# Cross attention with both query blocks side by side, and expert weights split into low parts and fetched in smaller steps

## The chip, the cores and the metric

The kernel runs on one core of a Trainium2 chip. The metric is the device time of one launch in microseconds (us). The core has five engines with a queue each: PE (TensorE, matrix products and transposes), DVE (VectorE), ACT (ScalarE), POOL (GpSimd) and SP (SyncE, which here only issues DMAs). Every engine works its queue in the written order and waits on semaphores.

## The reference

One decoder layer on x of 16 sequences x 256 rows x 256 columns, all in float32. It has three parts, each followed by a layer norm: a linear attention with decay, a cross attention against 77 context rows, and a mixture of experts in which every row uses 2 of 8 experts.

```python
x = _layernorm(x + _L0_attn_ref(x, ...))
x = _layernorm(x + _L0_xattn_ref(x, ctx_1024, ctx_1024, mask, ...))
x = _layernorm(x + _L0_ffn_ref(x, router_w, gate_w, gate_b, up_w, up_b, down_w, down_b))

...
scores = jnp.einsum('bhqd,bhkd->bhqk', qh, kh) * scale
scores = jnp.where(mask[:, None, :, :] == 0, jnp.float32(-1000000000.0), scores)
probs = jax.nn.softmax(scores, axis=-1)
out = jnp.einsum('bhqk,bhkd->bhqd', probs, vh)
...
g = jnp.einsum('nd,edf->nef', xf, gate_w) + gate_b
u = jnp.einsum('nd,edf->nef', xf, up_w) + up_b
h = jax.nn.silu(g) * u
expert_out = jnp.einsum('nef,efd->ned', h, down_w) + down_b
y = jnp.einsum('ne,ned->nd', probs, expert_out)
```

## The kernel before

The program has five stages that follow one another: `linear_attention` (to about 750 us), `cross_attention` (to about 1036 us), `route_tokens`, `run_experts` (about 1070 to 1475 us) and `combine`. The order of the work is written by hand: in each stage every engine has a function `sequence` or `tile` that says in which order it takes its steps, and semaphores tie the engines together. The change touches two stages.

**cross_attention.** One turn of `sequence(b, ...)` works on one of 16 sequences b, and each sequence has two blocks of 128 query rows (`blk` 0 and 1). The work of a sequence is spread over neighbouring turns. The steps for one block, and the engine that does them:

- PE `turn_x1` transposes the input rows and ACT `keep_xT` (L992) copies the result out of PSUM. PE `project_q` (L1242) makes the queries, ACT `keep_q` (L999) keeps them.
- PE `score` (L1258) makes the scores of one block in `ps_s`, of which there is one buffer. DVE `keep_scores` takes them out in four operations (L1125), adding the mask, and takes the row maximum (L1131).
- POOL `shift` (L955) subtracts the maximum, ACT `exponentials` (L1005) takes exp, DVE `sums` (L1136, L1138) makes the sum and its reciprocal, POOL `weigh` (L960) multiplies by it. All four pass over 128 x 1232 numbers. POOL also makes the mask bias (`mask_to_bias`, L947).
- PE `turn_probs` (L1273) transposes the ten chunks of the block in groups 0, 1 and 2 of 4, 4 and 2 chunks, through two PSUM buffers, and ACT `keep_pT` (L1014) copies each group.
- For both blocks at once: PE `weigh_values` (L1286), ACT `keep_oT` (L1021), PE `project_o` (L1294), DVE `add_residual` and `statistics`, ACT `normalise` (L1026 to L1040), PE `turn_x2` (L1305), ACT `keep_x2T` (L1048), PE `route` (L1312), ACT `keep_logits` (L1052).

Before the change the two blocks are half a turn apart: block 0 of sequence b+1 goes through score, shift and exp in turn b, block 1 in turn b+1. SP's `load_k`, `load_x`, `load_mask`, `load_v`, `store_x2` and `load_residual` are issued once a turn and are not touched.

**run_experts.** The rows are sorted by expert into tiles: 16 tiles of 512 rows, then 7 of 256 rows, the short tiles. Each tile has one expert. float32 products are made of three products of high and low parts, so each weight matrix is split: ACT `gu_high` (L1777) copies gate and up into the high part, POOL `low_parts` (L1757) subtracts it from the raw weights (128 x 2048 numbers, two SBUF inputs). ACT `dn_high` and DVE `dn_low` do the same for the down weights, ACT `x_high` and DVE `x_low` (L1833) for the input rows, ACT `hid_high` and DVE `hid_low` (L1868, two SBUF inputs) for the hidden layer. In tile t, PE does `gate_up(t, 0)` and `gate_up(t, 1)` (L1934), `down(t-1)` (L1946), `turn_x(t+1)` (L1923), `gate_up(t, 2)` and `gate_up(t, 3)`. `gate_up(t+1, 0)` waits for `low_parts` and `x_low` of tile t+1.

There are two buffers of raw weights. In tile t SP waits until both low parts of tile t are made, then reads the number of the expert of tile t+2 from a table (`experts`, L1694 and the value loads behind it), and then issues three loads of 512 KB (L1701 twice, L1703), which all count up one semaphore. `gu_high` waits for all three:

```python
act.wait_ge(w_loaded[par], 16 * W_LOADS * (turn + 1))
```

Of the kernel before, what the change touches and what calls it, by code (L numbers as in the profile page):

```python
# [14 lines left out]
P = 128  # L15
# [724 lines left out]
def cross_attention(nc, sh, cross, x1_dram, x1_bo_dram, mask, x2_dram, x2_all, logits_all):  # L740
# [18 lines left out]
    with ExitStack() as ctx:  # L759
# [165 lines left out]
        def _(pool):  # L925
# [49 lines left out]
            shift(0, 0, 0)  # L975
            all_sequences(pool, sequence)

        @block.scalar
        def _(act):
# [74 lines left out]
            def sequence(b, par, turn):  # L1054
                if has(b, 1):
                    keep_xT(b + 1)
                if has(b, -1):
                    keep_pT(b - 1, 1 - par, 1, (0, 1))
                if has(b, -2):
                    normalise(b - 2)  # L1060
                if has(b, -1):
                    keep_pT(b - 1, 1 - par, 1, (2,))
                if has(b, 1):
                    keep_q(b + 1)
                exponentials(b, par, 1)
                if has(b, -1):
                    keep_oT(b - 1)
                keep_pT(b, par, 0, (0, 1))
                if has(b, -2):
                    keep_x2T(b - 2)  # L1070
                keep_pT(b, par, 0, (2,))
                if has(b, -2):
                    keep_logits(b - 2)
                if has(b, 1):
                    exponentials(b + 1, 1 - par, 0)
# [8 lines left out]
            exponentials(0, 0, 0)  # L1084
            all_sequences(act, sequence)
            keep_pT(B - 1, (B - 1) % 2, 1, range(NG))
            normalise(B - 2)
            keep_x2T(B - 2)
            keep_logits(B - 2)
            keep_oT(B - 1)  # L1090
# [5 lines left out]
        def _(vec):  # L1096
# [75 lines left out]
            for c in range(1, B // SEQS):  # L1172
                for t in range(KC):
                    keep_k(c, t)
            all_sequences(vec, sequence)
# [4 lines left out]
        def _(pe):  # L1180
# [135 lines left out]
            def sequence(b, par, turn):  # L1316
                if has(b, 1):
                    turn_x1(b + 1)
                if has(b, -1):
                    turn_probs(b - 1, 1 - par, 1, (0, 1))  # L1320
                if has(b, 1):
                    project_q(b + 1)
                if has(b, -1):
                    turn_probs(b - 1, 1 - par, 1, (2,))
# [3 lines left out]
                turn_probs(b, par, 0, (0, 1))  # L1328
                if has(b, -2):
                    turn_x2(b - 2)  # L1330
                turn_probs(b, par, 0, (2,))
                if has(b, -1):
                    project_o(b - 1)
                if has(b, -2):
                    route(b - 2)
                if has(b, 1):
                    score(b + 1, 1 - par, turn + par, 1)
# [795 lines left out]
```

## Time and profile before

| what | us |
|---|---|
| median of 3 runs | 1579.49 |
| lowest and highest | 1578.34, 1579.90 |
| the profiled execution | 1584.93 |
| its span, first to last instruction | 1583.2 |

Over the span PE is busy for 83%, PE's weight loads 71%, DVE 55%, ACT 56% and POOL 45%. The profiled execution is one more run of the same program. A row of the timeline gives the start, the time in us, the engine, the line, the operation, what it writes and reads, and how many instructions are merged in it; in brackets stands how long the engine was idle before it, and what ended that. PE's matmuls overlap, so how long PE spends on a step is best read from one step's start to the next one's.

### The profile page before, as it was taken

What the parts mean: (1) busy time and instruction counts of PE and PEld (TensorE: products, weight loads), DVE (VectorE), ACT (ScalarE), POOL (GpSimd) and SP (SyncE); (2) the same over time, 40 slices, a digit from 0 to 9 for tenths busy, and PEclk for the clock granted to TensorE, in tenths of its full rate; (3) what the DMA queues carried; (4) which work ended last, traced back from release to release, by engine and by line L of the source; (5) the groups of instructions that cost most, each with busy time, mean ns of one, the idle gap of its engine ahead of it and who ended that gap; (6) DMA issues with size and microseconds to landing.
All of it is one profiled execution on the core that took longest, in us unless ns stands there. A gap on an engine that the chain in (4) does not pass through costs nothing. (4 is left out here: it accounts for less than half of the span.)

```text
span 1583.2 us, 30994 instructions
## 1 busy us (share of the span) xinstructions
PE 1321.9 (83%) x10439; PEld 1119.0 (71%) x10439; DVE 874.0 (55%) x1806; ACT 887.7 (56%) x2018; POOL 713.8 (45%) x792
## 2 busy tenths in 40 slices
PE   5999999999999999997879889713899999998100
PEld 4788888888888888885667667503789888888100
DVE  3345455545444545554577787567455555566446
ACT  4677777777777777775256666500454554555101
POOL 2244444444444444445266666401544445354564
PEclk9999999999999999998889999955899999999655
DMA  3300000000000000001133332202444544555333
GB/s 126 75 15 28 21 28 28 28 22 28 28 18 25 28 21 28 21 22 48 51 74 82 102 99 75 76 13 91 143 144 160 174 153 139 176 175 147 93 117 122
DMA packets 127907, 120.61 MB, mean 76 GB/s; under 512 B 42498, under 2 KB 108650, under 8 KB 127786
## 3 DMA queue, kind: packets, MB, share of 16 engines
q1 hardware_dynamic: 120970, 100.42, 20.7%
q0 software_dynamic: 6816, 18.62, 4.3%
q8 instruction: 70, 1.15, 0.3%
q14 instruction: 51, 0.42, 0.1%
HBM read 83.93 MB, written 28.26 MB: 71 GB/s over the span
## 5 line engine op out<-in xcount | busy, mean ns | idle before, releaser
L293 POOL TENSOR_SCALAR_AFFINE_SELECT a_decay<-a_decay 128x256 f32<-128x256 f32 x256 | 114.7, 452 | 260.6 <-ACT a_decay L373 258.9
L496 DVE TENSOR_TENSOR a_probs<-a_ps_s,a_decay 128x384 f32<-128x384 f32 x256 | 131.5, 552 | 158.5 <-PE a_ps_o L676 147.4
L302 POOL TENSOR_TENSOR a_key_sum<-a_probs 128x256 f32<-128x256 f32 x128 | 94.2, 736 | 170.3 <-DVE a_probs L496 158.2
L336 ACT ACTIVATE a_qk_exp<-a_ps_qk 128x512 f32<-128x512 f32 x128 | 76.5, 598 | 137.9 <-PE a_ps_qk L582 130.5
L582 PE MATMUL a_ps_qk<-a_xT_hi,a_w_hi 128*128 128x256 f32 x512 | 144.7, 283 | 3.6 <-ACT a_qk_relu L337 3.6
L582 PE MATMUL a_ps_qk<-a_xT_hi,a_w_lo 128*128 128x256 f32 x512 | 143.9, 281 | 0.0
L582 PE MATMUL a_ps_qk<-a_xT_lo,a_w_hi 128*128 128x256 f32 x512 | 143.7, 281 | 0.0
L1757 POOL TENSOR_TENSOR e_gu_lo<-e_gu_raw,e_gu_hi 128x2048 fp32r<-128x2048 f32 x23 | 106.4, 4627 | 81.8 <-ACT e_gu_hi L1777 81.8
L489 DVE SCALAR_TENSOR_TENSOR a_qk<-a_qk_exp,a_qk_relu 128x512 f32<-128x512 f32 x128 | 89.0, 695 | 97.4 <-ACT a_qk_relu L337 97.4
L657 PE MATMUL a_ps_s<-a_qk 64*128 64x256 f32 (+1 forms) x1024 | 132.2, 338 | 0.7 <-DVE a_probs L496 0.4
L1750 POOL DMA_INDIRECT e_x_in<-x_rows,e_index x78 | 74.8, 959 | 121.2 <-DVE e_index L1853 104.2
L371 ACT ACTIVATE a_decay<-a_ps_c,a_c_now 128x256 f32<-128x256 f32 x256 | 124.2, 485 | 2.4 <-PE a_ps_c L647 1.5
L1804 ACT CAST e_hid_hi<-e_hid 128x512 fp32r<-128x512 f32 (+1 forms) x92 | 49.1, 554 | 126.1 <-PE e_ps_y L1946 84.0
L670 PE MATMUL a_ps_o<-a_probs,a_values 128*64 128x256 f32 (+1 forms) x1024 | 111.5, 339 | 0.4 <-DVE a_probs L496 0.4
L657 PEld LDWEIGHTS a_ps_s<-a_qk 64*128 64x128 f32 x1024 | 107.8, 187 | 2.5 <-issue 2.4
L582 PEld LDWEIGHTS a_ps_qk<-a_xT_hi,a_w_hi 128*128 128x128 f32 x512 | 97.7, 191 | 5.4 <-issue 5.3
L955 POOL TENSOR_TENSOR b_probs<-b_probs,b_top 128x1232 f32<-128x1232 f32 x32 | 72.6, 2269 | 62.4 <-DVE b_top L1131 62.3
L373 ACT ACTIVATE a_decay<-a_ps_c,a_c_now 128x128 f32<-128x128 f32 x256 | 98.2, 384 | 0.0
L582 PEld LDWEIGHTS a_ps_qk<-a_xT_hi,a_w_lo 128*128 128x128 f32 x512 | 98.1, 192 | 0.0
L582 PEld LDWEIGHTS a_ps_qk<-a_xT_lo,a_w_hi 128*128 128x128 f32 x512 | 97.8, 191 | 0.1
L1862 DVE SCALAR_TENSOR_TENSOR e_hid<-e_ps_u,e_bias,e_gate 128x512 f32<-128x512 f32 (+1 forms) x92 | 61.1, 669 | 63.3 <-ACT e_gate L1798 55.3
L307 POOL TENSOR_TENSOR a_oT_lo<-a_oT,a_oT_hi 128x256 fp32r<-128x256 f32 x128 | 93.9, 734 | 1.2 <-ACT a_oT_hi L390 1.2
(282 smaller groups left out, 4024.3 us busy)
## 6 DMA issues: line engine op xcount, KB each, us to landing
e_gu_raw<-in_L_ffn_gate_w SPq DMA_DIRECT2D x23, 512.0 KB
e_gu_raw<-in_L_ffn_up_w SPq DMA_DIRECT2D x23, 512.0 KB
e_dn_raw<-in_L_ffn_down_w SPq DMA_DIRECT2D x23, 512.0 KB
y_sorted<-e_y_out SPq DMA_DIRECT2D x16, 512.0 KB
a_x_in<-in_x SPq DMA_DIRECT2D x16, 256.0 KB, 2.7
a_x_res<-in_x SPq DMA_DIRECT2D x16, 256.0 KB, 2.7
x_rows<-a_x SPq DMA_DIRECT2D x16, 256.0 KB, 2.1
x_bo_rows<-a_x_bo SPq DMA_DIRECT2D x16, 256.0 KB, 2.1
```

The source lines that it names most:

```text
L293: pool.affine_select(out=d, in_=d, compare_op=ALU.is_ge, fill=0.0, base=0, pattern=[[0, 2], [1, P]], channel_multiplier=-1)\
L302: pool.tensor_tensor(key_sum[:], probs[:, :, P:N], probs[:, :, N:TRI], ALU.add).then_inc(keys_summed, 1)
L307: pool.tensor_tensor(oT_lo[g % 2][:], oT[g % 2][:], oT_hi[g % 2][:].bitcast(F32), ALU.subtract).then_inc(oT_lo_done, 1)
L336: act.activation(qk_exp[:], ps_qk[:], ACT.Exp)
L371: act.activation(decay[h][:, 0:N], ps_c[:, h, :], ACT.Exp, bias=c_now[:, 0, head:head + 1], scale=-1.0)
L373: act.activation(decay[h][:, N:TRI], ps_c[:, h, P:N], ACT.Exp, bias=c_now[:, 1, head:head + 1], scale=-1.0).then_inc(decay_exp[h], 1)
L489: vec.scalar_tensor_tensor(qk[g][:], qk_exp[:], 1.0, qk_relu[:], ALU.min, ALU.add).then_inc(qk_done, 1)
L496: vec.tensor_tensor(probs[:, h, :], ps_s[h][:, 0:TRI], decay[h][:], ALU.mult)\
L582: mm = pe.matmul(out, l, r, start=(n == 0), stop=(n == len(todo) - 1))
L657: mm = pe.matmul(ps_s[h][:, out], qk[g][rows, 1, j], qk[g][rows, 0, i], start=True, stop=True)
L670: pe.matmul(out[h][:, 0, cols], values[par][:, j, 2 * g + h, :], probs[:, h, keys], start=(j == 0), stop=(j == 1), skip_group_check=True)
L1757: pool.tensor_tensor(gu_lo[par][:], gu_raw[par][:], gu_hi[par][:].bitcast(F32), ALU.subtract)\
```

## The change

In `cross_attention` both blocks of a sequence take each softmax step in the same turn, one right behind the other. `shift(b+1, 0)` and `shift(b+1, 1)` stand behind `weigh(b, 1)` on POOL, both `exponentials(b, ...)` stand in turn b on ACT, both `keep_scores(b+1, ...)` stand together on DVE. PE and ACT get a new order, in which the transposes of a block's probabilities are cut at another place, and `project_o(b-1)` stands between the two `score` steps. At the end of the stage `project_o(B-1)` and `keep_oT(B-1)` move ahead of the last steps of sequence B-2.

In `run_experts` the low parts of gate and up are made in four operations of 128 x 512, the table is read ahead of the waits, gate and up are loaded after their own low part is made and down after its own, and gate/up and down have semaphores of their own. `dn_high` now waits for the down weights. The pieces of the diff below are, in this order: POOL's and DVE's turn in the cross attention, PE's end of that stage, and in `run_experts` POOL's low parts, SP's tile, and ACT's two copies.

```diff
             def sequence(b, par, turn):
-                shift(b, par, 1)
                 weigh(b, par, 0)
                 weigh(b, par, 1)
                 if has(b, 1):
                     shift(b + 1, 1 - par, 0)
+                    shift(b + 1, 1 - par, 1)
                 if has(b, 2):
                     mask_to_bias(b + 2, par)
...
             def sequence(b, par, turn):
-                keep_scores(b, par, 1)
                 sums(b, par, 0)
                 sums(b, par, 1)
                 if has(b, 1):
                     keep_scores(b + 1, 1 - par, 0)
+                    keep_scores(b + 1, 1 - par, 1)
...
             turn_probs(B - 1, (B - 1) % 2, 1, range(NG))
             weigh_values(B - 1, (B - 1) % 2, (B - 1) // 2)
+            project_o(B - 1)
             turn_x2(B - 2)
             route(B - 2)
-            project_o(B - 1)
...
-                pool.tensor_tensor(gu_lo[par][:], gu_raw[par][:], gu_hi[par][:].bitcast(F32), ALU.subtract)\
-                    .then_inc(gu_lo_done[par], 1)
+                for k in range(KC):
+                    for cols in (slice(0, FF), slice(FF, 2 * FF)):
+                        ins = pool.tensor_tensor(gu_lo[par][:, k, cols], gu_raw[par][:, k, cols],
+                                                 gu_hi[par][:, k, cols].bitcast(F32), ALU.subtract)
+                ins.then_inc(gu_lo_done[par], 1)
...
                 if has(t, 2):
+                    e_next, e = experts(t, 1, 2, t + 2)
                     sp.wait_ge(gu_lo_done[par], turn + 1)
+                    load_gate_up(e, par)
                     sp.wait_ge(dn_lo_done[par], turn + 1)
-                    e_next, e = experts(t, 1, 2, t + 2)
-                    load_weights(e, par)
+                    load_down(e, par)
...
-                act.wait_ge(w_loaded[par], 16 * W_LOADS * (turn + 1))
+                act.wait_ge(gu_loaded[par], 16 * GU_LOADS * (turn + 1))
...
+            def dn_high(t, par, turn):
+                act.wait_ge(dn_loaded[par], 16 * (turn + 1))
```

PE's queue for one whole turn of the cross attention, before. `b_ps_m` takes `turn_x1`, `project_q`, `turn_x2` and `route`, `b_ps_s` the scores, `b_ps_t` the transposed probabilities (of block 0 or 1), `b_ps_o` first `weigh_values` and then `project_o`:

```order
L1235 MATMUL b_ps_m<-ident,b_x_in 128x128 x4
L1273 MATMUL b_ps_t<-ident,b_probs_1 128x128 x8
L1242 MATMUL b_ps_m<-b_xT,b_wT 128x256 x4
L1273 MATMUL b_ps_t<-ident,b_probs_1 128x128 x2
L1286 MATMUL b_ps_o<-b_pT,b_v_now 64x256 x12
L1258 MATMUL b_ps_s<-b_k_now,b_qT 128x154 x8
L1273 MATMUL b_ps_t<-ident,b_probs_0 128x128 x8
L1305 MATMUL b_ps_m<-ident,b_x 128x128 x4
L1273 MATMUL b_ps_t<-ident,b_probs_0 128x128 x2
L1294 MATMUL b_ps_o<-b_wT,b_oT 128x256 x4
L1312 MATMUL b_ps_m<-b_rwT,b_x2T 128x8 x4
L1258 MATMUL b_ps_s<-b_k_now,b_qT 128x154 x8
```

The same turn of PE's queue now:

```order
L1275 MATMUL b_ps_t<-ident,b_probs_1 128x128 x4
L1237 MATMUL b_ps_m<-ident,b_x_in 128x128 x4
L1275 MATMUL b_ps_t<-ident,b_probs_1 128x128 x6
L1244 MATMUL b_ps_m<-b_xT,b_wT 128x256 x4
L1288 MATMUL b_ps_o<-b_pT,b_v_now 64x256 x12
L1260 MATMUL b_ps_s<-b_k_now,b_qT 128x154 x8
L1296 MATMUL b_ps_o<-b_wT,b_oT 128x256 x4
L1275 MATMUL b_ps_t<-ident,b_probs_0 128x128 x4
L1260 MATMUL b_ps_s<-b_k_now,b_qT 128x154 x8
L1307 MATMUL b_ps_m<-ident,b_x 128x128 x4
L1275 MATMUL b_ps_t<-ident,b_probs_0 128x128 x6
L1314 MATMUL b_ps_m<-b_rwT,b_x2T 128x8 x4
```

The count of matmuls is the same. All transposes of block 1 of the sequence before now stand ahead of `project_q`, and the score of block 1 stands in the middle of the turn instead of at its end, with `project_o` between the two scores.

ACT's queue in the first part of a turn, before (`b_pT` is `keep_pT`, 4x128 or 2x128 by group; the rows to L1040 are `normalise`):

```order
L992 COPY b_xT<-b_ps_m 128x512
L1014 COPY b_pT<-b_ps_t 128x4x128 x2
L1026 ACTIVATE b_ln_var<-b_mv,b_eps_col 128x2
L1028 ACTIVATE b_rstd<-b_ln_var 128x2
L1030 ACTIVATE b_minus_rstd<-b_rstd 128x2
L1033 ACTIVATE b_shift<-b_mv,b_minus_rstd 128x1 x2
L1040 ACTIVATE b_x<-b_resid,b_shift,b_rstd 128x256 x2
L1014 COPY b_pT<-b_ps_t 128x2x128
L999 ACTIVATE b_qT<-b_ps_m,b_bq_col 128x256 x2
L1005 ACTIVATE b_probs_1<-b_probs_1 128x16x77
L1021 COPY b_oT<-b_ps_o 128x512
```

And now:

```order
L1015 COPY b_pT<-b_ps_t 128x4x128
L993 COPY b_xT<-b_ps_m 128x512
L1015 COPY b_pT<-b_ps_t 128x4x128
L1006 ACTIVATE b_probs_0<-b_probs_0 128x16x77
L1015 COPY b_pT<-b_ps_t 128x2x128
L1006 ACTIVATE b_probs_1<-b_probs_1 128x16x77
L1000 ACTIVATE b_qT<-b_ps_m,b_bq_col 128x256 x2
L1022 COPY b_oT<-b_ps_o 128x512
L1027 ACTIVATE b_ln_var<-b_mv,b_eps_col 128x2
```

Both exps stand between the copies of the transposed probabilities and `keep_q`; `normalise` moved from ahead of `keep_q` to behind `keep_oT`. Before, the exp of block 0 was the last step of the turn before.

## Rows read from the trace of the kernel before

**Rows 1.** Busy time by stretch, two turns of cross attention: us, engines (instructions), PEclk, DMA, GB/s

```profile
870.50:885.00 14.50, 12.13 (x109) 9.36 (x104) 11.00 (x20) 9.29 (x20) 9.76 (x5) 1.00 0.34 94
885.00:899.85 14.85, 12.93 (x103) 9.79 (x103) 10.96 (x19) 9.58 (x21) 9.79 (x6) 0.89 0.32 91
```

**Rows 2.** Timeline of PE over one turn of cross attention: start, us, step

```profile
914.46 0.81 PE L1258 MATMUL b_ps_s<-b_k_now,b_qT 32*128 32x154 f32 x16
...
918.44 1.99 PE L1242 MATMUL b_ps_m<-b_xT,b_wT 128*128 128x256 f32 x8 [1.71 <-ACT b_xT L992]
...
920.58 3.04 PE L1286 MATMUL b_ps_o<-b_pT,b_v_now 128*64 128x256 f32 x24
923.55 0.81 PE L1258 MATMUL b_ps_s<-b_k_now,b_qT 32*128 32x154 f32 x16
...
925.90 1.89 PE L1294 MATMUL b_ps_o<-b_wT,b_oT 128*128 128x256 f32 x8
...
928.51 0.81 PE L1258 MATMUL b_ps_s<-b_k_now,b_qT 32*128 32x154 f32 x16
```

**Rows 3.** PE's waits in ten turns: total us, times, longest us

```profile
PE b_ps_m L1242 <- ACT b_xT L992: 16.2, 10, 2.2
```

**Rows 4.** Costliest groups of cross attention: busy us, mean ns, idle before

```profile
L955 POOL TENSOR_TENSOR b_probs<-b_probs,b_top 128x1232 f32<-128x1232 f32 x32 | 72.6, 2269 | 62.4 <-DVE b_top L1131 62.3
L1125 DVE SCALAR_TENSOR_TENSOR b_probs<-b_ps_s,b_mask_bias 128x308 f32<-128x308 f32 x128 | 52.1, 470 | 9.2 <-PE b_ps_s L1258 5.4 <-PE b_ps_t L1273 2.5 <-issue 0.6
...
L1131 DVE TENSOR_REDUCE b_top<-b_probs 128x16 f32<-128x1232 f32 x32 | 45.9, 1436 | 1.1
...
L1005 ACT ACTIVATE b_probs<-b_probs 128x1232 f32<-128x1232 f32 x32 | 39.9, 1246 | 43.8 <-POOL b_probs L955 43.8
...
L999 ACT ACTIVATE b_qT<-b_ps_m,b_bq_col 128x256 f32<-128x256 f32 x32 | 13.4, 470 | 3.3 <-PE b_ps_m L1242 3.3
```

**Rows 5.** Timeline: second score of sequences 1 and 15, PE at the end

```profile
797.61 1.64 DVE L1125 SCALAR_TENSOR_TENSOR b_probs<-b_ps_s,b_mask_bias 128x308 f32<-128x308 f32 x4
...
1004.10 1.63 DVE L1125 SCALAR_TENSOR_TENSOR b_probs<-b_ps_s,b_mask_bias 128x308 f32<-128x308 f32 x4
...
1017.84 2.81 PE L1286 MATMUL b_ps_o<-b_pT,b_v_now 128*64 128x256 f32 x24
...
1023.72 3.50 PE L1294 MATMUL b_ps_o<-b_wT,b_oT 128*128 128x256 f32 x8 [0.75 <-ACT b_oT L1021]
```

**Rows 6.** Timeline of PE: starts of short tiles 17, 18 and 22

```profile
1400.99 0.36 PE L1934 MATMUL e_ps_g<-e_xT_hi,e_gu_hi 128*128 128x256 f32 x1
...
1412.60 0.55 PE L1934 MATMUL e_ps_g<-e_xT_hi,e_gu_hi 128*128 128x256 f32 x1 [2.44 <-DVE e_hid L1862]
...
1458.33 0.36 PE L1934 MATMUL e_ps_g<-e_xT_hi,e_gu_hi 128*128 128x256 f32 x1 [2.56 <-DVE e_hid L1862]
```

**Rows 7.** Timeline of short tile 17: SP, ACT, POOL, DVE

```profile
1404.29 0.75 SPq L1694 DMA_DIRECT2D e_where<-tile_table  x1
1407.53 0.39 SPq L1701 DMA_DIRECT2D e_gu_raw<-in_L_ffn_gate_w  x1
...
1404.00 1.91 ACT L1777 CAST e_gu_hi<-e_gu_raw 128x2048 fp32r<-128x2048 f32 x1 [1.39 <-DMA e_dn_raw<-in_L_ffn_down_w]
...
1406.09 4.61 POOL L1757 TENSOR_TENSOR e_gu_lo<-e_gu_raw,e_gu_hi 128x2048 fp32r<-128x2048 f32 x1 [4.04 <-ACT e_gu_hi L1777]
...
1407.77 3.56 DVE L1868 TENSOR_TENSOR e_hid_lo<-e_hid,e_hid_hi 128x256 fp32r<-128x256 f32 x2
```

**Rows 8.** Timeline of POOL: two operations back to back

```profile
889.96 2.27 POOL L955 TENSOR_TENSOR b_probs<-b_probs,b_top 128x1232 f32<-128x1232 f32 x1 [1.85 <-DVE b_top L1131]
892.19 2.27 POOL L960 TENSOR_TENSOR b_probs<-b_probs,b_rden 128x1232 f32<-128x1232 f32 x1
```

**Rows 9.** The page's costliest groups: a POOL operation of 256 columns

```profile
L302 POOL TENSOR_TENSOR a_key_sum<-a_probs 128x256 f32<-128x256 f32 x128 | 94.2, 736 | 170.3 <-DVE a_probs L496 158.2
```

**Rows 10.** Timeline of DVE ahead of the first tile

```profile
1085.72 6.26 DVE L1899 TENSOR_SCALAR e_col_hot<-e_count,slot_col,e_number 128x78 fp32r<-128x78 f32 x8
```

More of the change, by code:

```diff
@@ L975, in _ @@
             shift(0, 0, 0)
+            shift(0, 0, 1)
             all_sequences(pool, sequence)
@@ L1054, in sequence @@
             def sequence(b, par, turn):
+                if has(b, -1):
+                    keep_pT(b - 1, 1 - par, 1, (0,))
                 if has(b, 1):
@@ L1057, in sequence @@
                 if has(b, -1):
-                    keep_pT(b - 1, 1 - par, 1, (0, 1))
+                    keep_pT(b - 1, 1 - par, 1, (1,))
+                exponentials(b, par, 0)
+                if has(b, -1):
+                    keep_pT(b - 1, 1 - par, 1, (2,))
+                exponentials(b, par, 1)
+                if has(b, 1):
+                    keep_q(b + 1)
+                if has(b, -1):
+                    keep_oT(b - 1)
                 if has(b, -2):
                     normalise(b - 2)
[L1061 to L1068, printed above, removed]
+                keep_pT(b, par, 0, (0,))
                 if has(b, -2):
                     keep_x2T(b - 2)
-                keep_pT(b, par, 0, (2,))
+                keep_pT(b, par, 0, (1, 2))
                 if has(b, -2):
                     keep_logits(b - 2)
-                if has(b, 1):
-                    exponentials(b + 1, 1 - par, 0)
             keep_xT(0)
@@ L1083, in _ @@
             keep_q(0)
-            exponentials(0, 0, 0)
             all_sequences(act, sequence)
             keep_pT(B - 1, (B - 1) % 2, 1, range(NG))
+            keep_oT(B - 1)
             normalise(B - 2)
@@ L1089, in _ @@
             keep_logits(B - 2)
-            keep_oT(B - 1)
             normalise(B - 1)
@@ L1174, in _ @@
                     keep_k(c, t)
+            keep_scores(0, 0, 1)
             all_sequences(vec, sequence)
@@ L1316, in sequence @@
             def sequence(b, par, turn):
+                if has(b, -1):
+                    turn_probs(b - 1, 1 - par, 1, (0,))
                 if has(b, 1):
@@ L1327, in sequence @@
                     score(b + 1, 1 - par, turn + par, 0)
-                turn_probs(b, par, 0, (0, 1))
+                if has(b, -1):
+                    project_o(b - 1)
+                turn_probs(b, par, 0, (0,))
+                if has(b, 1):
+                    score(b + 1, 1 - par, turn + par, 1)
                 if has(b, -2):
                     turn_x2(b - 2)
-                turn_probs(b, par, 0, (2,))
-                if has(b, -1):
-                    project_o(b - 1)
+                turn_probs(b, par, 0, (1, 2))
                 if has(b, -2):
                     route(b - 2)
-                if has(b, 1):
-                    score(b + 1, 1 - par, turn + par, 1)
             turn_x1(0)
@@ L1731, in _ @@
             e0, e1 = experts(0, 0, 2, 1)
-            load_weights(e0, 0)
-            load_weights(e1, 1)
+            load_gate_up(e0, 0)
+            load_down(e0, 0)
+            load_gate_up(e1, 1)
+            load_down(e1, 1)
             sp.wait_ge(table_ready, 1)
@@ L1814, in tile @@
                     x_high(t + 1, 1 - par)
-                    dn_high(t + 1, 1 - par)
+                    dn_high(t + 1, 1 - par, turn + par)
                 for f in range(2, FC):
@@ L1822, in _ @@
             gu_high(0, 0, 0)
-            dn_high(0, 0)
+            dn_high(0, 0, 0)
             x_high(0, 0)
```

15 lines of the change are left out of this document (7 added, 8 removed).

## The prediction

> **What bounds the kernel now.** I began with the busy time by stretch. PE is filled in the linear attention and in the tiles of 512 rows. It is not filled in the cross attention and in the short tiles, which are the two places the change touches. In the cross attention a turn takes 14.5 us, or 14.85 us where the granted clock of the stretch is 0.89, while DVE works 11.0 us, POOL 9.8 and ACT 9.3 to 9.6 of it [rows 1]. So no engine is full, and a chain across engines must set the turn. PE's own timeline shows how much PE needs. From one second score to the next are 928.51 - 914.46 = 14.05 us, of which 1.71 us are a wait [rows 2]. What is left is 12.34 us: 2.27 (score, input rows, 8 transposes), 2.14 (queries, 2 transposes), 2.97 (values), 2.35 (score, 10 transposes, x2), 2.61 (output projection, routing). The wait is on `keep_xT`, and it stands in each of ten turns, 16.2 us in all [rows 3]. `keep_xT` is not late by itself: it stands on ACT behind the exp of block 0, which waits for POOL's `shift`, which waits for DVE's maximum [rows 4].
>
> In the short tiles PE starts tile 17 at 1400.99 and tile 22 at 1458.33, 57.34 / 5 = 11.47 us a tile [rows 6]. PE works 1412.60 - 2.44 - 1400.99 = 9.17 us of tile 17 and then waits. Three things are late in it [rows 7]. ACT's `gu_high` waited 1.39 us for the last weight load, the down weights, which it does not read. SP issued the loads only 3.24 us after it asked for the expert's number (1404.29 to 1407.53). And two `hid_low` operations took 3.56 us: they ended when POOL's `low_parts` had ended (1406.09 + 4.61 = 1410.70), and `x_low`, for which PE waits, stands behind them on DVE. The row at PE names DVE's `e_hid`; the semaphores behind it are those of `x_low`.
>
> **Cross attention, the new turn.** No instruction is added. I followed the new queues through two turns with the durations of the rows. Two limits compete.
>
> The first is the softmax loop, from the score of block 0 through both blocks to the score of the next sequence: score 0.81 [rows 2], DVE block 0 1.63 [rows 5] and 1.44, DVE block 1 again 3.07, `shift` of block 1 2.27, its exp 1.25, `keep_q` 2 x 0.47 [rows 4]. The sum is 11.4 us; I put some 0.1 us on each hand-over, about 11.9. Sums and reciprocals run beside the other block, and DVE's 11.0 us of work also fit. POOL's mask now stands between `shift` and `weigh`, 0.8 us that lie under DVE's sums.
>
> The second is PE's 12.34 us. It is larger, so PE should become the bound. What hides PE's former wait: ACT now copies the input rows ahead of the exps, and the six transposes of groups 1 and 2 stand between `turn_x1` and `project_q`. What is late next: `project_o` asks for `keep_oT` right behind the score, `project_q` for `keep_xT`, `route` for `keep_x2T`, and the last values for the copy of group 2, behind one exp. I count 0.05 to 0.1 us at each, 0.3 together, which makes 12.65. `keep_q` is queued behind two exps, but PE has 2.97 us of values to do meanwhile. SP's queue is not touched: its 12 value loads wait for `weigh_values` once a turn, as before, and in rows 3 no DMA is among what PE waits for.
>
> The clock: in a stretch at 0.89 a turn that PE bounds would grow by 12.34 x (1/0.89 - 1) = 1.5 us. In the view of rows 1 such turns are four of thirteen, and in the one shown PE works more, not less, than its neighbour. I take half as many, since PE will pause less, 0.2 us a turn. So 12.8 us a turn, bounded by 12.34 (no wait at all) and 13.8 (the waits that I count as covered come out at half of what goes away now).
>
> Before, the second scores of sequences 1 and 15 stand 1004.10 - 797.61 = 206.5 us apart, 14.75 a turn [rows 5]. Saved: 14 x (14.75 - 12.8) = 27.3 us (13.3 to 33.7). The first turns stay: `keep_q` of sequence 1 comes some 3 us later, but DVE is not free for the score before about then.
>
> At the end of the stage the last `project_o` starts at 1023.72, though its input was there at 1017.84 + 2.81 = 1020.65 plus a copy [rows 5]. It can start 2.4 us earlier. The `normalise` behind it now meets that of sequence 14 on ACT. I take 2 us (0 to 3).
>
> **Experts.** Four operations in place of one: 2048 columns cost 4.61 [rows 7], 256 columns 0.736 [rows 9], so 2.16 ns a column and 0.18 us each. A piece is 1.29 us, four are 5.16: 0.55 us more on POOL. In the large tiles nothing waits for it. There the change is at nothing, as long as DVE's `hid_low` does not meet POOL.
>
> In a short tile `gu_high` could start at 1404.00 - 1.39 = 1402.61, 1.6 us into the tile [rows 7]. Then 1.91 for the copy, 0.18 to POOL, 5.16: the low parts are ready 8.9 us into the tile, or 9.7 if DVE's two operations cut in between. That is near PE's 9.17. The other path: `hid_low` comes 1407.77 - 1400.99 = 6.8 us into the tile, and waits for one piece or two rather than for all. Unheld it would end at about 7.6, at the latest with POOL's last piece at 9.7. From its end to PE's next tile it was 1412.60 - 1411.33 = 1.27 us, so 8.9 to 11.0. The number's 3.2 us of reading fall away ahead of the loads, so these go out that much earlier. I take 9.8 us a tile, the middle of the two paths: 5 x (11.47 - 9.8) = 8.3 us, bounded by 9.17 (11.5 us) and by 11.0 (2.3 us).
>
> The Trainium skill speaks for and against this. Its page "SBUF — State Buffer" (section "SBUF: two separate sides") says that GpSimd and a DVE operation with two SBUF inputs take a shared port pair as an exclusive lock for a whole instruction. The 3.56 us of rows 7 agree. By that rule four instructions give four places to get in, which is the forecast. Its page "GPSIMD Engine Reference" (section "2.1 Instruction dispatch") says that a core begins the next instruction as soon as it has done its share of the last. If so the pair might never be let go between pieces, which is the second rival below. By the first page the time is the forecast's, by the second that rival's.
>
> Ahead of the first tile DVE's eight small operations took 6.26 us under the first `low_parts` [rows 10]. They would be held 0.6 us longer by four pieces, and this chain sets the first tile: -0.3 to +0.9, I take +0.6.
>
> **Sum.** -27.3 - 2 - 8.3 + 0.6 = -37.0 us. The profiled execution took 1584.93, so 1547.9 for one like it. The median of the runs, 1579.49, lies 5.4 us below it, and 1579.49 - 37.0 = 1542.5.
>
> **Rivals.**
>
> 1. The hand-overs hold PE. If `keep_q` or `keep_oT`, behind two exps on ACT, is late, PE waits again and the turn stays at 13.8 us. For it: ACT works in order and now has both exps in one piece. Against it: the 2.97 us of values. Saved: 14 x 0.95 + 2 + 8.3 - 0.6 = 23.0, so 1556.5.
>
> 2. The pieces don't let DVE in. Two POOL operations follow one another without a gap: the second starts at 892.19, the first ends at 889.96 + 2.27 = 892.23 [rows 8]. If `hid_low` is held to the end of all four at 8.9, it ends 1411.33 - 1410.70 = 0.6 us later, and the tile takes 8.9 + 0.6 + 1.3 = 10.8 us. Experts then save 5 x 0.67 = 3.4 us rather than 8.3, and the time is 1547.4. The change would then not do what its split says, and only the earlier loads would pay.
>
> 3. Slower. PE is the bound, so its clock decides. The last output projection, at the lower level, took 3.50 us where one in the loop took 1.89 [rows 2, 5], so a whole turn at that level would take 12.34 x 0.85 = 10.5 us more. If 26% of the denser turns' time fell to it, a mean granted clock of 0.87, they would lose 14 x 0.26 x 10.5 = 38 us, the whole gain. That is the point from which it decides; at a mean of 0.84 the time is about 1587. Against it: the full-clock stretches of rows 1 have PE as busy as those at 0.89.
>
> 4. Both go better than I count: 12.4 us a turn, 9.2 a tile, 1579.49 - 32.9 - 2 - 11.4 + 0.6 = 1533.8.
>
> **How the numbers follow.** Forecast 0.50, rival 1 0.16, rival 2 0.16, rival 3 0.04, rival 4 0.11, and 0.03 for a turn that stays as it is. A difference of 0.2% (3 us) is about what a measurement of this kernel can tell from none. Faster by more: 0.94. Within: 0.02. Slower: 0.04. The range from 1532 to 1558 takes in the forecast, rivals 1, 2 and 4.
>
> **What would show it.** In the profile of the changed kernel, second scores of DVE 12.6 to 13.0 us apart, PE's wait on `keep_xT` gone or under 0.3 us a turn, and PEclk 0.95 or more in the stage. In the short tiles, starts 9.8 us apart, `gu_high` no longer released by a DMA, `hid_low` for two blocks under 2.5 us. Turns over 13.5 us mean that a chain I held covered is not, and PE's waits name it. `hid_low` at 3 us or more with four POOL pieces beside it means rival 2.

## The result and the profile after

The changed kernel took 1543.44 us (median of 4 runs, 1540.89 to 1545.17), the kernel before 1578.91 us (median of 4): a ratio of 0.9776, 95% interval 0.9758 to 0.9794, or 35.5 us less; the forecast was 37.0 us less. In a later comparison the ratio was 0.9763 (0.9749 to 0.9776), 37.0 us less.

The profiled execution took 1540.89 us, with a span of 1539.0. Against the span before, 1583.2, that is 44.2 us. Walking down both traces from mark to mark, the difference splits as follows.

| stretch | before | after | difference | forecast |
|---|---|---|---|---|
| second score of sequence 1 to that of sequence 15 | 206.5 | 176.6 | -29.9 | -27.3 |
| from there to the last logits | 31.3 | 28.0 | -3.3 | -2 |
| last logits to the first rows transposed for the experts | 75.7 | 75.4 | -0.4 | +0.6 (with the next row) |
| tile 0, first to third block of gate and up | 8.0 | 9.2 | +1.2 | |
| start of tile 17 to start of tile 22 | 57.3 | 52.0 | -5.3 | -8.3 |
| tile 22 to the last output of the experts | 15.5 | 15.1 | -0.4 | 0 |
| combine, which the change does not touch | 105.7 | 101.0 | -4.7 | 0 |
| ahead of the second score of sequence 1 | 797.6 | 796.2 | -1.4 | 0 |

The stretches that the table leaves out, from the third block of tile 0 to tile 17 above all, agree within 0.1 us. The last two rows can't be put down to the change (see the end). Without them the traces differ by 38.1 us.

**Cross attention.** Three turns by stretch in the changed kernel, and the whole stretch of 14 turns, with the columns of [rows 1] (us, then PE, PEld, DVE, ACT, POOL busy, the granted clock, the DMA share, GB/s):

```profile
858.91:871.61 12.70, 12.62 (x110) 9.61 (x109) 10.90 (x21) 9.69 (x21) 9.78 (x5) 1.00 0.40 107
871.61:884.28 12.67, 12.62 (x110) 9.61 (x109) 10.90 (x20) 9.80 (x21) 9.78 (x5) 1.00 0.40 108
884.28:896.96 12.68, 12.61 (x110) 9.61 (x109) 10.91 (x21) 9.69 (x21) 9.79 (x5) 1.00 0.40 108
796.24:972.88 176.64, 175.00 (x1489) 133.40 (x1490) 151.37 (x262) 133.10 (x283) 137.00 (x70) 0.99 0.37 99
```

PE is busy for 175.0 of 176.6 us. DVE and POOL work what they worked in [rows 1]; the turn around them is shorter, and no turn after the first falls to the lower clock that [rows 1] show at 0.89. PE's timeline over one turn shows no wait in brackets, where [rows 2] had 1.71 us:

```profile
880.20 0.81 PE L1260 MATMUL b_ps_s<-b_k_now,b_qT 32*128 32x154 f32 x16
880.95 1.99 PE L1296 MATMUL b_ps_o<-b_wT,b_oT 128*128 128x256 f32 x8
...
888.20 1.99 PE L1244 MATMUL b_ps_m<-b_xT,b_wT 128*128 128x256 f32 x8
890.13 2.81 PE L1288 MATMUL b_ps_o<-b_pT,b_v_now 128*64 128x256 f32 x24
892.87 0.41 PE L1260 MATMUL b_ps_s<-b_k_now,b_qT 32*128 32x154 f32 x4
```

From score to score it is 892.87 - 880.20 = 12.67 us. What is left of the waits stands at PE's weight loads. These are the totals over 820 to 970 us (us, times, longest us), against 16.2 us in ten turns of [rows 3]:

```profile
PEld b_ps_m L1244 <- ACT b_xT L993: 3.3, 12, 0.3
PEld b_ps_m L1314 <- ACT b_x2T L1049: 3.1, 12, 0.3
PEld b_ps_o L1296 <- ACT b_oT L1022: 2.1, 12, 0.2
```

**Short tiles.** Starts of tiles 17, 18, 19 and 22 on PE (answers to [rows 6]):

```profile
1367.29 0.36 PE L1946 MATMUL e_ps_g<-e_xT_hi,e_gu_hi 128*128 128x256 f32 x1
...
1377.70 0.36 PE L1946 MATMUL e_ps_g<-e_xT_hi,e_gu_hi 128*128 128x256 f32 x1 [1.35 <-DVE e_hid L1874]
...
1388.11 0.35 PE L1946 MATMUL e_ps_g<-e_xT_hi,e_gu_hi 128*128 128x256 f32 x1 [1.35 <-DVE e_hid L1874]
...
1419.29 0.36 PE L1946 MATMUL e_ps_g<-e_xT_hi,e_gu_hi 128*128 128x256 f32 x1 [1.28 <-DVE e_hid L1874]
```

That is 10.41 us a tile, where it was 11.47. PE still waits 1.35 us in each. Tile 18 on ACT, POOL and DVE (answers to [rows 7]):

```profile
1379.24 1.91 ACT L1788 CAST e_gu_hi<-e_gu_raw 128x2048 fp32r<-128x2048 f32 x1
...
1381.32 5.24 POOL L1767 TENSOR_TENSOR e_gu_lo<-e_gu_raw,e_gu_hi 128x512 fp32r<-128x512 f32 x4 [1.79 <-ACT e_gu_hi L1788]
...
1384.03 1.37 DVE L1880 TENSOR_TENSOR e_hid_lo<-e_hid,e_hid_hi 128x256 fp32r<-128x256 f32 x1
...
1385.07 1.49 POOL L1767 TENSOR_TENSOR e_gu_lo<-e_gu_raw,e_gu_hi 128x512 fp32r<-128x512 f32 x1
1385.33 1.52 DVE L1880 TENSOR_TENSOR e_hid_lo<-e_hid,e_hid_hi 128x256 fp32r<-128x256 f32 x1
...
1386.84 0.74 DVE L1845 TENSOR_TENSOR e_xT_lo<-e_ps_x,e_xT_hi 128x256 fp32r<-128x256 f32 x2
1387.50 0.47 DVE L1874 SCALAR_TENSOR_TENSOR e_hid<-e_ps_u,e_bias,e_gate 128x256 f32<-128x256 f32 x1
```

`gu_high` waits for nothing and starts 1.54 us into the tile. POOL's four pieces (one row together; the last of them also by itself, from 1385.07) end at 1382.6, 1383.9, 1385.1 and 1386.6. The first `hid_low` starts 0.2 us behind the second of these ends and is let go by the third, the second `hid_low` by the fourth; each ends 0.28 us behind the end that lets it go. Each takes 1.4 to 1.5 us instead of 0.43. Behind them stand `x_low` and `hidden(2)`, and PE starts 0.14 us after `hidden(2)` ends (1387.97 to 1388.11).

### The profile page after: what moved, and what is told of

Its sections match the earlier page's. It is cut to its first block and busy times, and to the rows that moved or that the text cites. A ratio compares the mean times of both kernels' runs of the same rounds, so it can differ in the third digit from the quotient of the medians.

```text
span 1539.0 us, 31104 instructions
## 1 busy us (share of the span) xinstructions
PE 1315.0 (85%) x10439; PEld 1110.6 (72%) x10439; DVE 873.6 (57%) x1806; ACT 890.7 (58%) x2018; POOL 726.5 (47%) x861
## 5 line engine op out<-in xcount | busy, mean ns | idle before, releaser
L1767 POOL TENSOR_TENSOR e_gu_lo<-e_gu_raw,e_gu_hi 128x512 fp32r<-128x512 f32 x92 | 117.3, 1305 | 72.2 <-ACT e_gu_hi L1788 72.2
L1874 DVE SCALAR_TENSOR_TENSOR e_hid<-e_ps_u,e_bias,e_gate 128x512 f32<-128x512 f32 (+1 forms) x92 | 61.0, 668 | 57.3 <-ACT e_gate L1810 45.7
```

The lines of the kernel that those rows point to most:

```text
L1767: ins = pool.tensor_tensor(gu_lo[par][:, k, cols], gu_raw[par][:, k, cols], gu_hi[par][:, k, cols].bitcast(F32), ALU.subtract)
```

## The experiments

Each kernel was compared with the kernel before on its own chip. Three groups of four shared a chip, on which the kernel before took 1565.99, 1567.81 and 1581.34 us. Between groups only ratios and stretches of the traces are compared. Unless said otherwise an edit is made in the changed kernel.

### The two parts alone

`cross_only` is the kernel before with the new `cross_attention`, `experts_only` the kernel before with the new `run_experts`.

> Only the cross attention is changed; the experts are those of the kernel before. Theory (the two parts do not touch each other): second scores of DVE 12.6 to 12.7 us apart, the end of the stage 3.3 us shorter, in all 33 us less than before in the median (about 1546), short tiles still 11.5 us a tile. Rival (the gain in the cross attention is partly given back in the experts when these stay as before, or the other way round): a saving under 30 us, and this kernel together with experts_only does not add up to the whole change.

> Only the experts are changed; the cross attention is that of the kernel before. Theory: short tiles 10.4 us apart rather than 11.47 (5 times 1.06 = 5.3 us), the first tile about 0.8 us later, so 4.5 us less than before (about 1574). Rival (the 4.7 us by which the combine was shorter in the trace of the changed kernel belong to the change, for instance through an earlier last store): 9 us less (about 1570), with the combine shorter in its trace too.

Measured: `cross_only` 1536.52 us, ratio 0.9811 (0.9795 to 0.9826), 29.5 us less; `experts_only` 1562.31 us, ratio 0.9971 (0.9960 to 0.9982), 3.7 us less. In the traces the turns of `cross_only` are 12.61 us, the stretch to the last logits is 28.2, and those logits come 32.5 us earlier than in `experts_only`, whose turns are 14.76 us. The two savings add up to 33.2 us, where the whole change saved 35.5 and 37.0. Each has some 2 us of uncertainty, so the times show no more than that the parts are independent within it; "under 30 us" was just met, but the sum does not fail. The traces are sharper. From the second score of sequence 1 to the last logits `cross_only` takes 204.7 us and the changed kernel 204.6; from there to the last output of the experts `cross_only` takes 438.3 us and the kernel before 438.4, `experts_only` 432.8 and the changed kernel 433.5, whose tile 0 is 1.0 us longer by the clock (see the end). The combine is 90.2 and 90.3 us in these two, so the 4.7 us are not an effect of the experts.

### What bounds the turn of the cross attention

`late_xT`, in ACT's turn:

```diff
                 if has(b, -1):
                     keep_pT(b - 1, 1 - par, 1, (0,))
-                if has(b, 1):
-                    keep_xT(b + 1)
                 if has(b, -1):
                     keep_pT(b - 1, 1 - par, 1, (1,))
                 exponentials(b, par, 0)
+                if has(b, 1):
+                    keep_xT(b + 1)
```

> The changed kernel with ACT's keep_xT (and the second copy of transposed probabilities ahead of it) put back behind the exp of block 0, the place it had before; both blocks stay side by side. Theory (PE's former wait went because the copy of the input rows left its place behind an exp): project_q waits for keep_xT again, 1.5 to 2 us a turn, and since PE is filled otherwise the turn goes from 12.6 to about 14.1 us: some 20 us slower than the changed kernel. Rival (it is the side-by-side softmax that shortens the turn, and this place only uses slack): turns under 13.3 us, less than 10 us slower.

Measured: 1587.64 us, ratio 1.0034 (1.0024 to 1.0043). One copy moved behind one exp takes back the whole gain and more: against 0.9763, 43 us. The wait is the expected one, the turn is longer than both theories said. Two neighbouring turns of its trace by stretch (us, PE busy, clock, DMA share, GB/s), and PE in the second of them:

```profile
875.30:889.96 14.66, 12.62 (x110) 1.00 0.34 93
889.96:906.33 16.37, 14.28 (x110) 0.90 0.32 84
```

```profile
895.94 2.97 PE L1244 MATMUL b_ps_m<-b_xT,b_wT 128*128 128x256 f32 x8 [2.07 <-ACT b_xT L993]
898.84 3.47 PE L1288 MATMUL b_ps_o<-b_pT,b_v_now 128*64 128x256 f32 x24
```

With the clock at full speed the turn is 12.62 us of work and 2.0 of waiting. In 8 of the 14 turns the clock falls to its lower level behind the wait: from the start of the queries to the score it is then 6.30 us (895.94 to 902.24) against 4.67 in the changed kernel. From its second score of sequence 1 to that of sequence 15 there are 218.1 us, 15.6 a turn, and 14 x (15.6 - 12.6) = 42 us is nearly the whole loss. So a wait of PE costs its length and, in such turns, 1.6 us more. It also shows that the blocks' standing side by side is not enough for the gain: with it, and the copy in its old place, the turn is longer than before. Whether it is needed is not shown: no run moves the copy alone, in the kernel before.

`pe_less` leaves out half of the products in two of PE's steps:

```diff
-                    for k in range(KC):
-                        mm = pe.matmul(ps_m[:, t, :], wqT[:, k, t * P:(t + 1) * P], xT[:, k, :],
-                                       start=(k == 0), stop=(k == KC - 1))
+                    mm = pe.matmul(ps_m[:, t, :], wqT[:, 0, t * P:(t + 1) * P], xT[:, 0, :], start=True, stop=True)
...
-                    for k in range(KC):
-                        mm = pe.matmul(ps_lg[:, blk, :], x2T[:, k, blk * P:(blk + 1) * P], rwT[:, k, :],
-                                       start=(k == 0), stop=(k == KC - 1))
+                    mm = pe.matmul(ps_lg[:, blk, :], x2T[:, 0, blk * P:(blk + 1) * P], rwT[:, 0, :], start=True, stop=True)
```

> The changed kernel with half of the products of project_q and of route left out (only the first half of the contraction is summed), 1.4 us of PE's work a turn; every copy and hand-over stays. Theory (PE is the bound, and the softmax loop of 11.4 to 11.9 us is next): the turn goes from 12.6 to 11.7 to 11.9 us, not to 11.2; 11 to 14 us faster than the changed kernel. Rival A (no loop is near, PE alone counts): 11.2 to 11.3 us. Rival B (the turn is already held by a chain across the engines): 12.4 us or more.

Measured: 1531.54 us, ratio 0.9676 (0.9661 to 0.9691), 13.8 us less than at 0.9763. PE's scores of block 0 in two turns:

```profile
885.36 0.41 PE L1258 MATMUL b_ps_s<-b_k_now,b_qT 32*128 32x154 f32 x4 [0.26 <-ACT b_qT L1000]
...
897.11 0.41 PE L1258 MATMUL b_ps_s<-b_k_now,b_qT 32*128 32x154 f32 x4 [0.34 <-ACT b_qT L1000]
```

They are 11.75 us apart, and PE now waits for `keep_q`, which stands behind both exps. The theory holds: PE is the bound at 12.67 us, and the softmax loop is the next one at 11.75. Work taken from PE pays for the first 0.9 us of a turn.

### The end of the stage

`end_old` has `project_o(B - 1)` on PE and `keep_oT(B - 1)` on ACT behind the steps of sequence B-2 again, as before the change.

> The changed kernel with the last project_o and keep_oT of the cross attention back behind turn_x2 and route of the sequence before. Theory (the end of the stage is a chain through the last output projection, and was shortened by moving it): from the last second score to the last logits 30 to 31.5 us rather than 28, so 2 to 3.3 us slower than the changed kernel. Rival (the end was shorter because the turns ahead of it are closer): 28 to 28.5 us, no difference.

Measured: 1548.16 us, ratio 0.9779 (0.9766 to 0.9793). The intervals overlap with that of the changed kernel, so the times don't decide. The trace does: from the last second score to the last logits it is 1003.98 - 974.09 = 29.9 us, 1.9 more than in the changed kernel and 1.4 less than before. PE's last `project_o`, whose steps are in the same order as before:

```profile
993.83 1.99 PE L1296 MATMUL b_ps_o<-b_wT,b_oT 128*128 128x256 f32 x8 [0.75 <-ACT b_oT L1022]
```

The move brings 1.9 us, a little less than the theory's 2. The other 1.4 are the clock: the same step behind the same wait of 0.75 us took 3.50 us in [rows 5], where the granted clock was 0.50, and takes 1.99 here at a granted clock of 1.00, as it does in the changed kernel.

### What the four pieces do

`one_piece` has the old single operation in `low_parts`; `eight_pieces` cuts each row of it into four instead of two:

```diff
-                    for cols in (slice(0, FF), slice(FF, 2 * FF)):
+                    for cols in (slice(n * FF // 2, (n + 1) * FF // 2) for n in range(4)):
```

> The changed kernel with low_parts again as one operation of 2048 columns; everything else stays changed. Theory (an operation of DVE is held until the POOL instruction under way ends, and the second hid_low meets the last piece anyway, so the four pieces hardly help and only the earlier gu_high does): POOL runs from 3.6 to 8.2 us into a tile, both hid_low end at 8.9, and a short tile takes 10.1 to 10.2 us: 1 us faster than the changed kernel over five tiles, up to 1.5. Rival (the split brings the gain, as the sum of the prediction has it): a tile of 11 us or more, 3 us or more slower than the changed kernel.

> The changed kernel with low_parts in eight operations of 256 columns. Theory (one operation of DVE gets in at each boundary): each of the two held hid_low takes 0.4 to 1.1 us rather than 1.4 to 1.5, both end near 7.6 us into a tile, and what is last is POOL's own end at 3.6 + 8 x 0.74 = 9.5: tiles 9.5 to 9.8 us apart, 3 to 4 us faster than the changed kernel. Rival (DVE is not let in but only slowed while POOL works, so the size of a piece does not matter): hid_low stays at 1.4 us each, and the tile at 10.4 or above, since POOL works longer: same time or 1 us slower.

Measured: `one_piece` 1527.35 us, ratio 0.9749 (0.9736 to 0.9762); `eight_pieces` 1523.76 us, ratio 0.9731 (0.9718 to 0.9744). One tile of `one_piece` on POOL, DVE and PE:

```profile
1380.86 4.62 POOL L1765 TENSOR_TENSOR e_gu_lo<-e_gu_raw,e_gu_hi 128x2048 fp32r<-128x2048 f32 x1 [1.79 <-ACT e_gu_hi L1785]
...
1383.58 2.18 DVE L1877 TENSOR_TENSOR e_hid_lo<-e_hid,e_hid_hi 128x256 fp32r<-128x256 f32 x1
...
1385.69 0.41 DVE L1877 TENSOR_TENSOR e_hid_lo<-e_hid,e_hid_hi 128x256 fp32r<-128x256 f32 x1
...
1387.37 0.36 PE L1943 MATMUL e_ps_g<-e_xT_hi,e_gu_hi 128*128 128x256 f32 x1 [1.06 <-DVE e_hid L1871]
```

The first `hid_low` is held to POOL's end (1385.48), the second runs free. The tile takes 10.13 us (1377.24 to 1387.37), 0.28 less than with four pieces. In the short tiles the split into four costs time rather than bringing it. In `eight_pieces` two held `hid_low` take 1.59 us together, 0.72 and 0.95 us for the two:

```profile
1377.11 5.96 POOL L1767 TENSOR_TENSOR e_gu_lo<-e_gu_raw,e_gu_hi 128x256 fp32r<-128x256 f32 x8 [1.09 <-ACT e_gu_hi L1788]
...
1380.18 1.59 DVE L1880 TENSOR_TENSOR e_hid_lo<-e_hid,e_hid_hi 128x256 fp32r<-128x256 f32 x2
...
1380.87 0.33 PE L1935 MATMUL e_ps_x<-ident,e_x_in 128*128 128x128 f32 x1 [1.22 <-DMA e_x_in<-x_rows,e_index]
```

The time that DVE is held goes with the size of a piece (up to 2.2 us with 2048 columns, 1.4 to 1.5 with 512, 0.7 to 1.0 with 256). In all three kernels a held `hid_low` ends 0.28 us behind the end of a piece, so it waits for an end and is not slowed.

The expected tile of 9.5 to 9.8 us did not come: the transposes of rows of the successive tiles are 11.2, 9.1, 11.0 and 9.0 us apart, 10.05 on the mean. A new wait took the place of the old, for the rows that POOL gathers, in every second tile. From issue to landing (least, median, most of two gathers), for the gathers ahead of the wait shown, issued at 1373.8 and 1375.1, and for the next two, at 1383.2 and 1384.5:

```profile
DMA to landing us min/median/max: 2.7/4.2/5.8
...
DMA to landing us min/median/max: 3.1/3.4/3.6
```

In the tile of the wait shown the second gather takes 5.8 us, and 5.6 in the other waiting tile. In the two waiting tiles of the trace it is issued 0.9 and 1.3 us into the tile, where the changed kernel issues it at 0.9, so POOL's 0.7 us of longer work explains little of the wait. What differs is that the next weights' loads are issued 1.0 us behind the slow gather (at 1376.1) and 1.8 us behind the other (at 1386.3). That they slow it is likely, but not shown.

`eight_pieces` is nevertheless the faster one, 0.9731 against 0.9763. From the last logits to the last output its trace is 5.2 us shorter than the first one of the changed kernel: 0.4 up to the first rows, 1.4 by the clock of tile 0 (see the end), and 3.4 from tile 17 on.

### What the loads do

`old_loads` keeps four pieces and puts the waits and loads back:

```diff
                 if has(t, 2):
-                    e_next, e = experts(t, 1, 2, t + 2)
                     sp.wait_ge(gu_lo_done[par], turn + 1)
-                    load_gate_up(e, par)
                     sp.wait_ge(dn_lo_done[par], turn + 1)
+                    e_next, e = experts(t, 1, 2, t + 2)
+                    load_gate_up(e, par)
                     load_down(e, par)
...
                 act.wait_ge(gu_loaded[par], 16 * GU_LOADS * (turn + 1))
+                act.wait_ge(dn_loaded[par], 16 * (turn + 1))
```

> The changed kernel with SP's tile as before (both waits, then the table is read, then all three loads), and gu_high waiting for all three loads; low_parts stays in four pieces. Theory (the earlier gu_high brings the gain): gu_high starts 2.5 to 3.0 us into a tile rather than 1.5, POOL ends at 10 or later, short tiles 10.9 to 11.4 us apart, 3 to 5 us slower than the changed kernel. Rival (the four pieces bring the gain, as the prediction's sum has it for half of it): tiles stay at 10.4 to 10.6, less than 1 us slower.

> The changed kernel itself, for comparison on the same chip as the others of this call. The trace should again show turns of 12.6 us and short tiles 10.41 us apart. The two times in which the first two traces differ without a changed line behind them (the combine, 4.7 us shorter, and the stage ahead of the cross attention, 1.3 us) should not follow the change; the first tile of the experts, 1.2 us longer in the first trace of the changed kernel, shows here whether it is the change (again 9.2 us) or a clock that rose later (8.0 us as before).

Measured on one chip: `after_again` 1530.78 us, ratio 0.9763 (0.9749 to 0.9776); `old_loads` 1533.59 us, ratio 0.9783 (0.9768 to 0.9797). `gu_high` waits again for the down weights:

```profile
1378.53 1.92 ACT L1789 CAST e_gu_hi<-e_gu_raw 128x2048 fp32r<-128x2048 f32 x1 [0.63 <-DMA e_dn_raw<-in_L_ffn_down_w]
...
1390.55 1.91 ACT L1789 CAST e_gu_hi<-e_gu_raw 128x2048 fp32r<-128x2048 f32 x1 [1.69 <-DMA e_dn_raw<-in_L_ffn_down_w]
```

The transposes of rows in four short tiles stand 46.35 us apart, 11.6 us a tile, against 41.6 in `after_again`. `gu_high` starts 2.3 and 3.3 us into these two tiles, and POOL ends at 9.7 and 10.8. The loads are what shortens the tile; with the old loads and four pieces it is no shorter than the 11.47 us of [rows 6]. How much of it is the earlier issue and how much that `gu_high` waits for two loads only, was not tried apart. The gap from the last logits to the last output is 438.4 us against 433.8. The medians differ by less, 2.8 us, since `old_loads` reached the last logits 1.5 us sooner, where no line differs. The time alone would not decide, as the intervals overlap; the trace does. Tile 0 of `after_again` took 9.2 us again (see the end).

### The wait that is left, and a faster kernel

`hid_four` gives each block of hidden rows its own buffer, so that `hidden(2)` need not wait for `hid_low(0)`, and reorders DVE's tile:

```diff
-        hid = [sb(f"e_hid{n}", [P, T]) for n in range(2)]
+        hid = [sb(f"e_hid{n}", [P, T]) for n in range(FC)]
...
-                    vec.wait_ge(hid_lo_done[n], m)
+                    if not isinstance(m, int) or m > 1:
+                        vec.wait_ge(hid_lo_done[n], m - 1)
...
-                hid_low(0)
-                hid_low(1)
                 if has(t, 2):
                     tile_index(t + 2, par)
                 if has(t, 1):
                     x_low(t + 1, 1 - par)
-                for f in range(2, FC):
-                    hidden(f)
-                    hid_low(f)
+                hidden(2)
+                hid_low(0)
+                hid_low(1)
+                hidden(3)
+                hid_low(2)
+                hid_low(3)
```

`best` is the same with one operation for all `low_parts` but the first, which has eight; `best_two` has eight for the first and four for the others.

> The changed kernel with four buffers for the hidden rows instead of two, so that in DVE's queue x_low and hidden(2) no longer stand behind the two hid_low that POOL holds: x_low, hidden(2), hid_low(0), hid_low(1), hidden(3), hid_low(2), hid_low(3). Theory (PE's wait at the start of a short tile is for hidden(2), behind the held hid_low): PE's wait of 1.35 us goes, and its own work of 9.17 us or POOL's end at 8.9 sets the tile: 9.1 to 9.4 us, 5 to 6 us faster than the changed kernel. Rival (the gather of the rows or POOL's end is last next): 9.8 to 10.1 us a tile, 2 to 3 us faster.

> hid_four with low_parts in one operation for all tiles but the first, and in eight for the first, where DVE's small operations stand against it. Theory (one piece costs POOL 0.6 us less a tile, and nothing is held any more that PE waits for; at the start eight pieces hold DVE for 4.6 us rather than 5.9): as hid_four, and 1 to 2 us faster at the start of the experts. Rival (with one piece hid_low is late for the down projection of the next tile): tiles of 9.5 us or more, and no gain over hid_four.

> hid_four with the first low_parts in eight operations and all others in four. Theory: tiles of 9.1 to 9.2 us as in hid_four (four pieces let the cast of the indices and so the gather in early), and DVE held for 4.6 us at the start rather than 5.9: 1 to 1.5 us faster than hid_four and best, ratio to before about 0.971. Rival (what hid_four saves in the tiles and best at the start are the same microseconds): no difference.

Measured: `hid_four` 1524.55 us, ratio 0.9723 (0.9710 to 0.9736), 6.2 us less than the changed kernel on the same chip; `best` 1524.37, ratio 0.9720 (0.9707 to 0.9734); `best_two` 1540.30 against 1581.34 before, ratio 0.9724 (0.9709 to 0.9738). DVE in one tile of `hid_four`:

```profile
1392.63 1.25 DVE L1865 CAST e_index<-e_token 128x2 uint32<-128x2 f32 x1
1393.80 0.74 DVE L1845 TENSOR_TENSOR e_xT_lo<-e_ps_x,e_xT_hi 128x256 fp32r<-128x256 f32 x2
1394.96 0.48 DVE L1875 SCALAR_TENSOR_TENSOR e_hid<-e_ps_u,e_bias,e_gate 128x256 f32<-128x256 f32 x1 [0.42 <-ACT e_gate L1810]
1395.36 0.75 DVE L1881 TENSOR_TENSOR e_hid_lo<-e_hid,e_hid_hi 128x256 fp32r<-128x256 f32 x2
```

Both `hid_low` come behind POOL's end and run free (0.75 us for the two), `hidden(2)` waits only for its gate, and PE's wait at the start of the short tiles is gone: the transposes of rows are 9.04 to 9.40 us apart, 9.18 on the mean of four, which is PE's own work of 9.17. The first theory holds, and this kernel is faster than both. The edit also moves `x_low` ahead of the two `hid_low`; what the buffers bring without that, or that without them, was not tried. `best` has tiles of 9.46 us, PE waiting 0.40. At the start, eight pieces hold DVE's small operations for 4.59 us instead of 5.85, but also the next two rows of its queue, and the first rows are transposed only 0.3 us earlier. So neither variant beats `hid_four`.

## Why the prediction was right, and where not

**The turn: right.** The forecast was 12.65 us (12.34 of PE's work and 0.3 of hand-overs) and 0.2 for the clock. Undisturbed turns took 12.67. The hand-overs are the three weight-load waits shown above, 8.5 us in 12 turns or 0.7, most of it under the matmuls still running. The mean of 14 turns is 12.62, since the first is long (13.0) and the second short (11.7).

**The term for the clock was mis-sized.** I took half of the four disturbed turns of thirteen. None was left from the second turn on. This and the short second turn make the 2.6 us between -27.3 and -29.9. What I missed is that the dips followed PE's wait: `late_xT`, with a wait of 2.0 us, has them in 8 of 14 turns, and the changed kernel, with `keep_xT` down to 3.3 us in 12 turns, has none. The stretch ran at 0.99, as "0.95 or more" had it. The sum should have put them at zero along with the wait.

**The second bound: right.** The softmax loop was put at about 11.9 us; `pe_less` runs at 11.75. Rival 1, that `keep_q` behind two exps holds PE, was wrong for this kernel: the scores wait for values, not for queries. But it is only 0.9 us away.

**The end of the stage:** 3.3 us rather than 2, beyond the bound of 3. The moved step brings 1.9 of them, as forecast. The other 1.4 are the clock again: the sum had no term for the last `project_o` running at full clock, 1.99 us for 3.50 (`end_old`).

**The short tiles: right in sign, mis-sized.** The step that failed is "waits for one piece or two rather than for all". The other path of that sum was right: `gu_high` at 1.54 us into the tile for a forecast of 1.6, POOL's end at 8.86 for 8.9. `hid_low` came at 6.33, when pieces ended at 6.17, 7.42 and 8.86. There are two `hid_low`, and an end lets one in; so two ends had to pass, and the second was POOL's last. The held pair took 2.9 us, not under 2.5. The tile became 8.86 + 0.29 + 1.26 = 10.41 us, between the forecast of 9.8 and rival 2 with 10.8, and 5.3 us were saved rather than 8.3. The prediction's own numbers had most of it: with pieces of 1.29 us from 3.7 us on and `hid_low` at 6.8, the first is let go at 7.6, the second at 8.9, and 8.9 + 1.27 = 10.2. Instead I took 9.8 as the middle of 8.9 and 11.0, which is 9.95. The 0.8 us allowed for cut-ins were 0.2: POOL's four pieces took 5.24 us, and 5.05 in `hid_four`, where the `hid_low` come behind them.

**Rival 2** gave the better number for the tile (10.8) for a wrong reason. The pieces do let DVE in, as the Trainium skill, "SBUF — State Buffer" (section "SBUF: two separate sides"), would have it; each `hid_low` went at an end. The page "GPSIMD Engine Reference" of the Trainium skill (section "2.1 Instruction dispatch") did not decide here: the trace of `eight_pieces`, with 0.72 and 0.95 us, shows a place to get in between POOL's operations, though they follow without a gap.

**The reading of PE's wait was wrong.** I put it down to `x_low`, against the name in the row. PE starts 0.14 us after `hidden(2)`, and 0.53 us after `x_low`; the profile had the right one. `gate_up(t+1, 0)` waits not only for `low_parts` and `x_low`, but also until `hidden(2)` of tile t has emptied the PSUM buffers that it writes. The sum was not hurt, since both stand behind `hid_low` in one queue (0.74 and 0.47 us, together my 1.27), but the cure is another: `hidden(2)` waits for the buffer that `hid_low(0)` reads, and four buffers, with `x_low` moved ahead, were worth 6.2 us.

**The start of the experts:** DVE was held 5.85 us rather than 6.26, where I had 0.6 more. The first rows came 0.4 us earlier, just outside my range of -0.3 to +0.9.

**The total** of -37.0 came out at -35.5 and -37.0 in two comparisons, partly by luck, since the missing 3.0 us in the tiles stand against 3.9 more in the cross attention.

## What to carry over

Look for the engine that will be the bound next and add its own work from the timeline; the loop of the others is the second number, and both can be had from the trace of before within 0.2 us. A wait of the bounding engine costs more than its length where its clock falls behind it. Splitting an operation that holds another engine let in, in these traces, one waiting operation at each end, so count the waiting ones and when they come, and rather take them out of the queue ahead of what is waited for.

## What was not expected

**The clock of tile 0.** Between the first and the third block of gate and up, tile 0 took 7.7 to 9.3 us over the traces, by when the clock rose from its lower level of 1.2 to that of 2.4 GHz, about 3 to 6 us after the start; before that a matmul of 512 columns takes 0.63 us instead of 0.39. It was 8.0 us before, 8.1 in `experts_only`, 8.9 in `cross_only` and 9.2 in both traces of the changed kernel, but 7.7 in `old_loads` and 7.8 in `eight_pieces` and `best`, so it is no fixed price of either part. The +1.2 us of the table are this. What decides the moment stays open.

**The combine.** In the eight traces of the first two groups it took 90.2 to 90.7 us, in the four of the third 105.5 to 105.9 but for 104.4 in `pe_less`, and 101.0 and 105.7 in the first two traces. The first two groups ran on two chips and the third on another, all with the same code in this stage, so it goes with the chip; these 15 us are about what the kernel before differs by between the groups (1565.99 and 1567.81 against 1581.34). Of the first two traces the chip is not on record, and why they differ by 4.7 us stays open.

**Ahead of the cross attention.** The second score of sequence 1 stands at 794.8 to 798.0 us in twelve traces with the new cross attention, and at 797.2 and 797.6 in the two with the old. So the 1.4 us of the table are not shown to be the change's.

**Which operations of DVE are held.** A cast of 128 x 2 elements took 1.25 us beside POOL's pieces in `hid_four` (shown above); in the changed kernel, behind POOL's end, it took 0.15. The eight column operations at the start were held as well. Neither has two whole tensors as input (the column operations read one, and columns of scalars). The maximum in the cross attention is not held; here it runs under the end of a `shift` at its usual 1.44 us (changed kernel, POOL and DVE):

```profile
884.44 2.28 POOL L955 TENSOR_TENSOR b_probs<-b_probs,b_top 128x1232 f32<-128x1232 f32 x1 [0.99 <-DVE b_top L1132]
...
885.96 1.44 DVE L1132 TENSOR_REDUCE b_top<-b_probs 128x16 f32<-128x1232 f32 x1
```

The Trainium skill's page "SBUF — State Buffer" (section "SBUF: two separate sides") counts operations in a two-port mode among those that take the lock; no run here took such a mode away to see.
